# Second cross attention of a two-layer Perceiver: the sums' reciprocals as 16 columns, and the last key tile of each group summed in PSUM

## The reference

```python
qp = jnp.einsum('bld,ed->ble', q, Wq)
scores = jnp.einsum('bld,bmd->blm', qp, kv)
idx = jnp.argmax(scores, axis=-1)
mem = jnp.take_along_axis(kv, idx[..., None], axis=1)
mkv = jnp.einsum('bld,ed->ble', mem, Wkv)
mk, mv = jnp.split(mkv, 2, axis=-1)
qh = qp.reshape(b, l, h, dh).transpose(0, 2, 1, 3)      # 16 heads of 32
logits = jnp.einsum('bhld,bmd->bhlm', qh, mk) * scale
attn = jax.nn.softmax(logits, axis=-1)
out = jnp.einsum('bhlm,bmd->bhld', attn, mv)
```

## Time and profile before

| | |
|---|---|
| median of 3 runs | 1133.74 us (1131.56 to 1134.1) |
| span of the profiled execution, first to last instruction | 1129.8 us |
| TensorE busy | 1047.0 us, 93% |
| VectorE, ScalarE, GpSimd busy | 819.6, 489.2, 416.9 us |
| mean granted TensorE clock | 0.980 |

### The profile page before, as it was taken

One profiled execution on the slowest core, in us unless ns is written; L12 is line 12 of the kernel. 1 busy time (PEld: TensorE's weight loads), 2 busy tenths in 40 slices (PEclk: granted clock), 3 DMA queues, 4 the chain that ended last, 5 costly groups with the idle time before them and its releaser, 6 DMA issues.

```text
span 1129.8 us, 14853 instructions
## 1 busy us (share of the span) xinstructions
PE 1047.0 (93%) x4981; PEld 495.9 (44%) x4981; DVE 819.6 (73%) x1178; ACT 489.2 (43%) x731; POOL 416.9 (37%) x229
## 2 busy tenths in 40 slices
PE   7999999999999989999479999999997799888997
PEld 3444444444444444544134444444642145466453
DVE  5476666799999376685973399999477557476896
ACT  2345554666666537146771110100034615255163
POOL 5177778200000644000020377767128920084003
PEclk9999999999999999999779999999999999999998
DMA  6145545533433345320010435546100010000001
GB/s 237 75 132 194 184 160 166 201 112 121 147 140 112 142 157 224 111 93 1 0 75 6 148 142 200 188 170 188 37 1 1 8 70 1 1 1 1 2 1 38
DMA packets 41830, 112.64 MB, mean 100 GB/s; under 512 B 4512, under 2 KB 15296, under 8 KB 35648
## 3 DMA queue, kind: packets, MB, share of 16 engines
q1 hardware_dynamic: 38592, 101.13, 25.5%
q10 hardware_dynamic: 2880, 9.96, 2.6%
q0 software_dynamic: 320, 1.05, 0.3%
HBM read 103.18 MB, written 7.34 MB: 98 GB/s over the span
## 4 chain that ended last, share of the span: by engine, by line
PE 70%; DVE 17%; ACT 5%; issue 3%; DMA 2%; POOL 2%; DVEq 0%; SPq 0%; ACTq 0%; POOLq 0%
PE PS L773 5%; PE PS L1647 5%; PE PS L1649 5%; PE PS L775 5%; PE PS L1648 5%; PE PS L774 5%; PE PS L804 5%; PE PS L805 5%; PE PS L806 5%; PE PS L255 3%; PE PS L256 3%; PE PS L257 3%; DVE arena L1998 2%; DMA arena<-in_w 2%; DVE arena L1574 2%
## 5 line engine op out<-in xcount | busy, mean ns | idle before, releaser
L773 PE MATMUL PS<-arena 128*128 128x512 f16 x256 | 97.0, 379 | 2.0 <-DVE arena L622 2.0
L1647 PE MATMUL PS<-arena 128*128 128x512 f16 x256 | 97.0, 379 | 1.8 <-DVE arena L1531 1.8
L804 PE MATMUL PS<-arena 128*128 128x512 f16 x256 | 97.0, 379 | 0.9 <-DVE arena L695 0.9
L774 PE MATMUL PS<-arena 128*128 128x512 f16 x256 | 97.0, 379 | 0.0
L775 PE MATMUL PS<-arena 128*128 128x512 f16 x256 | 97.0, 379 | 0.0
L1648 PE MATMUL PS<-arena 128*128 128x512 f16 x256 | 97.0, 379 | 0.0
L1649 PE MATMUL PS<-arena 128*128 128x512 f16 x256 | 97.0, 379 | 0.0
L806 PE MATMUL PS<-arena 128*128 128x512 f16 x256 | 97.0, 379 | 0.0
L805 PE MATMUL PS<-arena 128*128 128x512 f16 x256 | 97.0, 379 | 0.0
L629 DVE TENSOR_TENSOR arena<-PS,arena 128x512 f32<-128x512 f32 x64 | 43.6, 681 | 58.0 <-ACT arena L553 58.0
L249 PE MATMUL PS<-IDENTB 128*128 128x512 bf16 x225 | 60.5, 416 | 21.9 <-DVE SM L1259 21.9
(11 more groups left out here) (370 smaller groups left out, 2439.8 us busy)
## 6 DMA issues: line engine op xcount, KB each, us to landing
arena<-in_ctxT SPq DMA_DIRECT2D x32, 1024.0 KB, 6.3
arena<-in_ctx SPq DMA_DIRECT2D x16, 1024.0 KB, 5.4
arena<-in_w ACTq DMA_DIRECT2D x8, 1024.0 KB, 5.2
arena<-in_w SPq DMA_DIRECT2D x8, 1024.0 KB, 4.8
XN<-in_ffnGU SPq DMA_DIRECT2D x16, 384.0 KB, 3.4
XN<-in_WinT SPq DMA_DIRECT2D x16, 290.0 KB, 5.1
gu_hi<-arena SPq DMA_DIRECT2D x16, 192.0 KB, 3.4
gu_lo<-arena SPq DMA_DIRECT2D x16, 192.0 KB, 3.5
```

The lines of the kernel that those rows point to most:

```text
L773: pe.matmul(bank, CHI[:, b, e, cols], QHI[:, e, :], start=(e == 0), stop=False)
L774: pe.matmul(bank, CHI[:, b, e, cols], QLO[:, e, :], start=False, stop=False)
L804: pe.matmul(PS[:, t, :], PHI[:, j, cols], CHI[:, b, j, :], start=False, stop=False)
L1647: pe.matmul(bank, QHI3[:, e, cols], CHI3[:, b, e, :], start=(e == 0), stop=False)
```

## The change

`sums` now has the second set of matmuls in every group, so GpSimd leaves out the additions of key tile 3 in groups 0 to 2 (8 a group in all groups). The copies of banks 7 and 6 go from VectorE to ScalarE (`take_group`, after the exp of unit 6). The long reciprocal of groups 0 to 2 is replaced: TensorE transposes DEN at unit 8 (`sum_columns`), so that each query row's sums of four heads stand in 16 distinct columns (4 tiles of 4 heads); VectorE takes their reciprocals and repeats each 32 times (`group_reciprocal`, after the entry of unit 9); TensorE turns them back into bank 7 at unit 11 (`spread_reciprocals`); VectorE multiplies after unit 12 (`group_scaled`). The last group keeps its form. ScalarE's waits for GpSimd change to fit, as unit 12 and on now wait for the sums of the group before. The list of marks (PE_MARK, DVE_MARK) gets the new names, not shown.

```diff
--- before.py
+++ after.py
...
@@ -1341,6 +1342,8 @@
         ATTT = view(138 * K, [DT, N])
         DEN = view(154 * K, [N])
         ACC = [view(86 * K, [4, N]), XT]
+        RDEN = view(174 * K, [NT, 4])
+        RSPREAD = view(156 * K, [NT, P])
 
         WINH = view(0, [4 * DT, QP], F16)
         WINL = view(18 * K + 512, [4 * DT, QP], F16)
@@ -1429,7 +1432,7 @@
         def added(n):
 
             g, m, j = n // 16, (n // 4) % 4, n % 4
-            return 12 * g + 4 * max(m - 1, 0) + j + 1
+            return 8 * g + 4 * max(m - 1, 0) + j + 1
 
         def shift_entry(g):
 
@@ -1468,7 +1471,7 @@
             pool.memset(MKS[96:98, :], MSHIFT).then_inc(pool_marks, 1)
             for n in range(UNITS):
                 g, m, j = n // 16, (n // 4) % 4, n % 4
-                if m == 0 or n >= UNITS - 4:
+                if m in (0, NT - 1):
                     continue
                 acc = ACC[g % 2][:, j, :]
                 pool.wait_ge(s3_p, n + 1)
@@ -1514,13 +1517,25 @@
                 act.activation(SHIFT[0:4, g, 0, :], PS[0:4, 2 * (e % 2), :], ACT.Copy,
                                scale=1.0 / MSHIFT).then_inc(s3_row_hi, 1)
 
+            def take_group(g):
+
+                act.wait_ge(pe_marks, PE_MARK[f"s3_sums{g}"])
+                act.copy(DEN, PS[:, 7, :]).then_inc(s3_den, 1)
+                act.wait_ge(s3_pv, 4 * g + 4)
+                act.copy(ATTT[:, g, :], PS[:, 6, :]).then_inc(s3_den, 1)
+
             shift_hi(0)
             for n in range(UNITS):
                 act.wait_ge(s3_logits, n + 1)
                 if n >= 16:
                     act.wait_ge(s3_pv, n // 4 - 3)
-                    act.wait_ge(s3_acc, added(n - 16))
+                    if n % 16 < 12:
+                        act.wait_ge(s3_acc, added(n - 16))
+                    elif n % 16 == 12:
+                        act.wait_ge(pe_marks, PE_MARK[f"s3_sums{n // 16 - 1}"])
                 act.activation(PT[:, n % 16, :], PS[:, 4 + n % 2, :], ACT.Exp).then_inc(s3_p, 1)
+                if n % 16 == 6 and n > 16:
+                    take_group(n // 16 - 1)
                 if n % 16 == 10 and n // 16 < GROUPS - 1:
                     shift_hi(n // 16 + 1)
             norm_act(act, 4)
@@ -1582,22 +1597,27 @@
                                          in1=SHIFT[0:4, g, 0, :], op0=ALU.mult, op1=ALU.subtract
                                          ).then_inc(s3_taken[e % 2], 1)
 
-            def weighted(g):
-
+            def group_reciprocal(g):
+
+                dve.wait_ge(pe_marks, PE_MARK[f"s3_cols{g}"])
+                link(dve.reciprocal(RDEN, PS[:, 7, :].rearrange("p (t j r) -> p t j r", t=NT, j=4)[:, :, :, 0]))
+                dve.tensor_copy(RSPREAD.rearrange("p t (j r) -> p (t j) r", j=4),
+                                RDEN.rearrange("p t j -> p (t j)").unsqueeze(2).to_broadcast([P, 4 * NT, DH])
+                                ).then_inc(dve_marks, 1)
+
+            def group_scaled(g):
+
+                dve.wait_ge(pe_marks, PE_MARK[f"s3_spread{g}"])
+                dve.wait_ge(s3_den, 2 * g + 2)
+                dve.tensor_tensor(ATTT[:, g, :], PS[:, 7, :], ATTT[:, g, :], ALU.mult).then_inc(s3_attt, 1)
+
+            def last_group():
+
+                g = GROUPS - 1
+                dve.wait_ge(pe_marks, PE_MARK[f"s3_sums{g}"])
+                link(dve.reciprocal(DEN, PS[:, 7, :]))
                 dve.wait_ge(s3_pv, 4 * g + 4)
-                dve.wait_ge(pe_marks, PE_MARK[f"s3_sums{g}"])
-                if g < GROUPS - 1:
-                    dve.tensor_copy(DEN, PS[:, 7, :]).then_inc(s3_den, 1)
-                    dve.tensor_copy(ATTT[:, g, :], PS[:, 6, :]).then_inc(s3_den, 1)
-                    dve.wait_ge(s3_den, 3 * g + 2)
-                    dve.reciprocal(DEN, DEN).then_inc(s3_den, 1)
-                    dve.wait_ge(s3_den, 3 * g + 3)
-                    dve.tensor_tensor(ATTT[:, g, :], ATTT[:, g, :], DEN, ALU.mult).then_inc(s3_attt, 1)
-                    dve.wait_ge(s3_attt, g + 1)
-                else:
-                    dve.reciprocal(DEN, PS[:, 7, :]).then_inc(s3_den, 1)
-                    dve.wait_ge(s3_den, 3 * g + 1)
-                    dve.tensor_tensor(ATTT[:, g, :], PS[:, 6, :], DEN, ALU.mult).then_inc(s3_attt, 1)
+                dve.tensor_tensor(ATTT[:, g, :], PS[:, 6, :], DEN, ALU.mult).then_inc(s3_attt, 1)
 
             def take_entry(e):
 
@@ -1616,9 +1636,11 @@
                 e = entry_at(n)
                 if e is not None:
                     take_entry(e)
-                if n % 16 == 6 and n > 16:
-                    weighted(n // 16 - 1)
-            weighted(GROUPS - 1)
+                if n % 16 == 9 and n > 16:
+                    group_reciprocal(n // 16 - 1)
+                if n % 16 == 12 and n > 16:
+                    group_scaled(n // 16 - 1)
+            last_group()
             for t in range(NT):
                 add_tile(dve, 3, t)
                 norm_tile(dve, 4, t).then_inc(ln_xn, 1)
@@ -1723,7 +1745,7 @@
                 if b == 0:
                     pe.wait_ge(s3_kv, 2)
                 if m == 0 and g:
-                    pe.wait_ge(s3_den, 3 * (g - 1) + 2)
+                    pe.wait_ge(s3_den, 2 * g)
                 for j in range(4):
                     ins = pe.matmul(PS[DH * j:DH * (j + 1), 6, :], MVAL[:, m, :], PT[:, (4 * b + j) % 16, :],
                                     start=(m == 0), stop=(m == NT - 1))
@@ -1731,17 +1753,30 @@
 
             def sums(g):
 
-                last = g == GROUPS - 1
-                pe.wait_ge(s3_acc, added(16 * g + (11 if last else 15)))
+                pe.wait_ge(s3_acc, added(16 * g + 11))
                 if g:
-                    pe.wait_ge(s3_den, 3 * (g - 1) + 1)
+                    pe.wait_ge(s3_attt, g)
                 for j in range(4):
-                    ins = pe.matmul(PS[DH * j:DH * (j + 1), 7, :], ONES[:, 0:DH], ACC[g % 2][:, j, :],
-                                    start=True, stop=not last)
-                if last:
-                    for j in range(4):
-                        ins = pe.matmul(PS[DH * j:DH * (j + 1), 7, :], ONES[:, 0:DH], PT[:, 12 + j, :],
-                                        start=False, stop=True)
+                    pe.matmul(PS[DH * j:DH * (j + 1), 7, :], ONES[:, 0:DH], ACC[g % 2][:, j, :], start=True, stop=False)
+                for j in range(4):
+                    ins = pe.matmul(PS[DH * j:DH * (j + 1), 7, :], ONES[:, 0:DH], PT[:, 12 + j, :],
+                                    start=False, stop=True)
+                ins.then_inc(pe_marks, 1)
+
+            def sum_columns(g):
+
+                pe.wait_ge(s3_den, 2 * g + 1)
+                for t in range(NT):
+                    cols = slice(t * P, (t + 1) * P)
+                    ins = pe.transpose(PS[:, 7, cols], DEN[:, cols], IDENT[:, :])
+                ins.then_inc(pe_marks, 1)
+
+            def spread_reciprocals(g):
+
+                pe.wait_ge(dve_marks, DVE_MARK[f"s3_rden{g}"])
+                for t in range(NT):
+                    ins = pe.matmul(PS[:, 7, t * P:(t + 1) * P], RSPREAD[:, t, :], IDENT[:, :],
+                                    start=True, stop=True)
                 ins.then_inc(pe_marks, 1)
 
             for e in range(FIRST):
@@ -1756,8 +1791,13 @@
                     e = entry_at(n)
                     if e is not None:
                         entry(e)
-                if n % 16 == 4 and 16 < n < UNITS:
-                    sums(n // 16 - 1)
+                if 16 < n < UNITS:
+                    if n % 16 == 4:
+                        sums(n // 16 - 1)
+                    if n % 16 == 8:
+                        sum_columns(n // 16 - 1)
+                    if n % 16 == 11:
+                        spread_reciprocals(n // 16 - 1)
                 if n >= 9 and n % 4 == 1:
                     weigh((n - 9) // 4)
             sums(GROUPS - 1)
```

More of the change, by code:

```diff
@@ L168, in marks @@
             return {name: n + 1 for n, name in enumerate(names)}
-        PE_MARK = marks("s0_turned", "s0_spread", "s0_close", "s0_den", "s1_mean", "s1_var", "s1_spread", "s3_sums0", "s3_sums1", "s3_sums2", "s3_sums3", "s4_dt_psum", "s4_sums", "s5_scale_psum")
-        DVE_MARK = marks("s0_mask", "s0_colmax", "s0_rden", "s1_rstd", "w_scale", "s3_memidx", "s4_dtb", "s4_dta", "s4_sums_read", "s4_la", "s4_parts", "s4_rms_early", "s4_rms_last", "s5_taps", "s5_scale",
+        PE_MARK = marks("s0_turned", "s0_spread", "s0_close", "s0_den", "s1_mean", "s1_var", "s1_spread", "s3_sums0", "s3_cols0", "s3_spread0", "s3_sums1", "s3_cols1", "s3_spread1", "s3_sums2", "s3_cols2",
+                         "s3_spread2", "s3_sums3", "s4_dt_psum", "s4_sums", "s5_scale_psum")
+        DVE_MARK = marks("s0_mask", "s0_colmax", "s0_rden", "s1_rstd", "w_scale", "s3_memidx", "s3_rden0", "s3_rden1", "s3_rden2", "s4_dtb", "s4_dta", "s4_sums_read", "s4_la", "s4_parts", "s4_rms_early", "s4_rms_last", "s5_taps", "s5_scale",
                           "s5_out_scale")
```

## The result

| | before | changed |
|---|---|---|
| median | 1133.8 us (1131.56 to 1134.1, 4 runs) | 1138.22 us (1137.66 to 1140.05, 4 runs) |
| ratio, 95% interval | | 1.0045 (1.0023 to 1.0067) |
| a second comparison | 1133.34 us (35 runs) | 1137.72 us (12 runs), 1.0038 (1.0024 to 1.0052) |
| span of the profiled execution | 1129.8 us | 1136.7 us |

What follows compares the result with a forecast made beforehand. TensorE was busy 93% of the span; in the second cross attention its queue waits on VectorE and GpSimd. Terms 0.87 + 0.24 - 0.56 + 1.6 + 0.6 = +2.75 us on 1133.74 gave 1136.5 us, range 1131.9 to 1139.9.

Steps and rivals of the forecast that it cites:

- the band that the forecast itself was given: Whole kernel: 1135.3 to 1138.0 us around the forecast of 1136.5 us, given chance 0.40.
- half-clock rival: TensorE idle before two spreads falls to half clock, some 1.4 us each: 1137.9 us for one, 1139.3 for two; chance 0.12.
- The spread in TensorE's queue: Groups 1 and 2, behind unit 11's logits: TensorE idle 2.3 to 2.8 us until VectorE's reciprocals, held behind shift_lo.
- The "faster" rival: VectorE has the reciprocals before TensorE reaches unit 11, saving two spread waits, 5.1 us: 1131.4 us; chance 0.14.
- Sums: Second set of matmuls in groups 0 to 2: 1.85 us for both sets, TensorE paying 0.85 us more three times.
- The sum over groups: Second cross attention: 0.87 + 0.24 - 0.56 + 1.6 + 0.6 = +2.75 us; groups about 20.3, 19.5 and 15.8 us.
- GpSimd's chain in group 3: Seven additions from the end of unit 5's exp, 8.7 us, ending at about +9.8 and just covered.
- 2.75: Forecast total of the changes in the second cross attention, in us, carried to the median for 1136.5 us.
- Port: VectorE's copy before both spreads waits a full GpSimd addition on the shared port: +1.0 us each, 1138.5 us; chance 0.12.
- the bound of 1.69: Upper bound on VectorE's copy before the spread: 0.42 + 1.27 us, if it waits a whole GpSimd addition.
- nothing outside the loop changes: The prediction held that nothing outside the 65 us of the second cross attention changes.

Runs made afterwards that it cites:

- the second profile: The changed kernel profiled again with no edit: loop 69.1 us with no half-clock stretch, median 1137.7 us, ratio 1.0038.
- copies on VectorE: Changed kernel with the copies of banks 7 and 6 back in VectorE's queue, behind the entry of unit 6: 1141.02 us, 1.0052.
- the reciprocals first: Changed kernel with VectorE's group_reciprocal moved ahead of unit 9's take_entry: 1128.77 us, ratio 0.9961.
- sums alone: Kernel before with the second set of sums matmuls in all groups, without the columns or ScalarE's copies: 1134.33 us, 1.0018.
- the reciprocals first and GpSimd's sums: Changed kernel with group_reciprocal ahead of unit 9's entry and GpSimd adding all key tiles as before: 1131.08 us, 0.9980.

## Why the prediction was right

The direction and the mechanism were right: the spread's wait outweighs all that the change saves. That the size is so near is in part luck, as said below. The measured 1138.2 us lies just above the band that the forecast itself was given (1135.3 to 1138.0), next to the half-clock rival (1137.9, chance 0.12).

- *The spread in TensorE's queue* was named as the place that decides, with its chain exp 10, shift_hi, shift_lo, reciprocal, copy. The waits were 2.12 and 2.55 us (foretold 2.3 to 2.8, so the first is a little short of it), there was none in group 3, and taking the chain apart at shift_lo gave the loop 4.3 us back. The "faster" rival put 5.1 us on exactly this, and a time of 1131.4 us; the kernel that does it measures 1128.8, of which a part lies outside the loop.
- *Sizes along the chain.* In brackets is what was foretold. The reciprocal of 16 columns took 0.23 us (0.25), the copy 0.70 (0.7), and the spread 1.0 at full clock, 887.90 to 888.90 in the second profile (0.9 to 1.05). From unit 5's logits to the spread it was 890.78 - 881.62 = 9.16 us (9.7). The forecast's excess of 0.5 us came in steps. The copies followed each other 0.47 us apart, not 0.5 to 0.6, so unit 9's logits came at +3.86 (+4.05). Unit 10's came 2.15 us behind them (2.35), at +6.0 (+6.4), 0.26 us later than before the change and not 0.65. The last 0.1 is in the steps from shift_hi to the spread, the last of which, from the copy's end to TensorE's start, took 0.06 us (0.1, for which there had been no row). The transposes took 0.66 us (0.45), but in the hole that the copies make, so they cost nothing.
- *Sums.* 879.76 to 881.62 is 1.86 us, as 1.85 foretold.
- *The sum over groups*, at full clock: group 1 took 19.71 us (20.3), group 2 19.12 (19.5), and group 3 0.4 more than before, up to the last reciprocal (0.84). GpSimd's chain in group 3 was covered, as foretold: it ended at 911.33 and the last sums began at 911.49.
- *What was off.* The sum counted the changed groups at full clock, but held them against a group 1 of before that had a half-clock stretch. With full clock on both sides it would have been 2.75 + 1.5 = 4.2 us in the loop, where 2.9 was measured. The two errors, 1.3 us too much for the work and 1.5 us too little for the clock, hid each other: that 2.75 came so near was luck. The half clock was a rival with 0.12; it should have been a part of the sum on either side, as it comes in some executions of both: 1, 0 and 2 stretches in three profiles of the changed kernel, 1, 0 and 1 in three of before, 1.5 to 1.6 us each (foretold 1.4).
- *Port.* A whole addition to wait for did not come about at either spread. The copy took 0.70 us where it takes 0.43 with no addition running at its start. The 0.27 are the rest of an addition: GpSimd's addition ended at 890.44 and the copy at 890.72. With the copies on VectorE an addition from 870.29 to 871.55 had begun just before the copy, which took 1.46 us and ended at 871.83, again 0.28 behind it. So the bound of 1.69 was no exaggeration, and that 0.7 was met hangs on where the additions happened to stand. This is what the Trainium skill says in "SBUF — State Buffer", section "Who interferes with whom": the second of the two waits until the first is done. The runs agree in both directions: with the reciprocals first, the copy began at 863.39 and GpSimd's addition at 863.42, and the addition took 1.53 us where its neighbours take 1.27.
- *The rest.* The time rose by 4.4 us, and 2.9 to 3.4 are shown in the loop. The rest, some 1 us, is inside the interval; where it lies is not shown. The prediction took it that nothing outside the loop changes. Behind the loop that held to 0.6 us for these two kernels, but not for the reciprocals first, where that part was 1.4 to 1.9 us shorter.

## What to carry to other kernels

When an engine's long instruction is broken up into a short one and two steps on another engine, the new waits go where the queues put them: look for what stands ahead of the short step in its own queue, and what stands behind its consumer. Here the reciprocal itself had become short, 0.23 us for 16 columns where 512 take 3.36. But one unrelated step (shift_lo) stood ahead of it and waited for a third engine, and so TensorE waited 2.1 to 2.6 us, twice. Two lines moved made 0.4% slower into 0.4% faster. Before a part of a profile is used as a base, see whether its clock is the same in a second execution: here one fall of the clock cost 1.5 us, half as much as the 2.9 us of the change.

## What the runs showed of the hardware that I had not expected

The same wait in the same kernel is followed by half clock in one execution and not in the next. The wait of 2.70 us was followed by it in two of three profiles of before, that of 2.12 us in one and that of 2.55 us in two of three of the changed kernel. Waits of 1.9 us were followed by it in none of four profiles (three of before, one of sums alone), but one of 1.57 us was, in the kernel with the reciprocals first and GpSimd's sums (half clock 891.0 to 894.4). The length of the wait alone doesn't tell. TensorE's work also ran at half clock ahead of the loop, with 2.30 us idle before it in every profile, in some executions and not in others.
